# Three attention layers on one core: row maxima split before their transpose, one DMA of eight rows a unit, fewer idle matmuls before the second layer

## What is computed

```python
# block 0 (heads of 16, positional bias added to the scores), then layer norm
attn = softmax(q * scale @ k + pos[..., :, None] + pos[..., None, :])
x = layer_norm(x + w_proj @ (attn @ v) + b_proj)
# blocks 1 and 2 (heads of 32), group norm first
xn = group_norm(x) * gamma + beta
attn = softmax((xn @ wq.T + bq) * scale @ (xn @ wk.T + bk))
x = x + wo @ (attn @ (xn @ wv.T + bv)) + bo
# block 3
V = (Wv @ x + bv) * sigmoid(mean(Q * K)); energy = V @ (Ws @ x + bs).T
x = x + softmax(energy) @ (We @ x + be)
```

## Time and profile before

| | us |
|---|---|
| three timed runs | 490.71, 485.31, 489.66 |
| their median | 489.66 |
| the profiled execution | 484.69 |
| its span, first to last instruction | 483.0 |
| PE busy in the span | 455.1 (94%) |
| DVE busy | 362.9 (75%) |
| ACT busy | 267.4 (55%) |
| POOL busy | 214.8 (44%) |
| mean granted TensorE clock (1 is full) | 0.987 |

### The profile page before, as it was taken

The page is one execution under the profiler, slowest core; times in us unless marked ns, Lnnn a source line. Parts: engine busy times, 40 slices in busy tenths (PEclk is TensorE's granted clock), DMA queues, the critical chain, the costliest instruction groups (busy, mean ns, idle before and its releaser), DMA issues.

```text
span 483.0 us, 7045 instructions
## 1 busy us (share of the span) xinstructions
PE 455.1 (94%) x2228; PEld 233.9 (48%) x2228; DVE 362.9 (75%) x700; ACT 267.4 (55%) x515; POOL 214.8 (44%) x195
## 2 busy tenths in 40 slices
PE   8898999999896989999899999999999999999996
PEld 6544444444246576544444433656544444433463
DVE  7699877876578489977776756769987776748673
ACT  3228877777622327876766672124777665765032
POOL 8300031047310005889788941002799789980100
PEclk9979999999998999999999999999999999999999
DMA  5331525103210154488954441045377865452002
GB/s 154 55 59 26 155 50 134 34 4 66 47 21 0 29 126 115 90 201 178 203 115 86 92 78 24 1 97 127 82 156 153 173 116 107 76 103 47 0 2 87
DMA packets 20657, 41.88 MB, mean 87 GB/s; under 512 B 7458, under 2 KB 8746, under 8 KB 20364
## 3 DMA queue, kind: packets, MB, share of 16 engines
q1 hardware_dynamic: 15324, 25.41, 22.0%
q0 software_dynamic: 5152, 16.00, 18.0%
q10 hardware_dynamic: 144, 0.02, 0.0%
HBM read 5.94 MB, written 1.05 MB: 14 GB/s over the span
## 4 chain that ended last, share of the span: by engine, by line
PE 69%; SPq 11%; DVE 7%; DMA 4%; ACT 4%; POOL 3%; issue 2%; ACTq 0%; DVEq 0%; POOLq 0%
PE S L983 16%; PE PV L1021 15%; PE S L1010 15%; SPq L338 5%; SPq L331 4%; DMA k_stack<-kL 3%; PE PV L935 3%; PE S L1145 3%; ACT E L589 3%; DVE max L734 3%; POOL SUMS L525 2%; PE M L1034 2%; PE PV L961 2%; PE S L1179 2%; PE S L961 2%
## 5 line engine op out<-in xcount | busy, mean ns | idle before, releaser
L734 DVE TENSOR_REDUCE max<-S 128x1 f32<-128x512 f32 x384 | 238.8, 674 | 11.0 <-PE S L983 10.6
L589 ACT ACTIVATE E<-S 128x512 f32<-128x512 f32 x384 | 210.7, 607 | 54.2 <-PE S L1010 46.4
L525 POOL TENSOR_TENSOR SUMS<-E 128x512 f32<-128x512 f32 x120 | 158.9, 1437 | 108.5 <-ACT E L589 108.2
L983 PE MATMUL S<-k_stack,q_stack 126*128 126x512 f32 x384 | 176.8, 474 | 8.0 <-DMA k_stack<-kL 5.6
L1010 PE MATMUL S<-q_stack,k_stack 128*128 128x512 f32 x384 | 155.1, 413 | 5.5 <-ACT E L589 4.6
L983 PEld LDWEIGHTS S<-k_stack,q_stack 126*128 126x128 f32 x384 | 72.8, 191 | 78.7 <-DVE max L734 48.7
L1021 PE MATMUL PV<-E,V 128*32 128x512 f32 x768 | 91.6, 598 | 0.0
L1010 PEld LDWEIGHTS S<-q_stack,k_stack 128*128 128x128 f32 x384 | 72.3, 190 | 34.6 <-ACT E L589 20.0
L747 DVE TENSOR_TENSOR mHL<-S,mHL 4x128 fp32r<-4x128 f32 x48 | 13.3, 278 | 48.8 <-ACT mHL L578 48.8
L1021 PEld LDWEIGHTS PV<-E,V 128*32 128x32 f32 x768 | 20.7, 109 | 46.5 <-issue 27.2
L578 ACT ACTIVATE mHL<-S 4x128 fp32r<-4x128 f32 x48 | 12.6, 263 | 49.9 <-PE S L1001 49.9
(11 more groups left out here) (174 smaller groups left out, 336.9 us busy)
## 6 DMA issues: line engine op xcount, KB each, us to landing
SUMS<-SUMS POOLq DMA_DIRECT2D x30, 512.0 KB, 6.0
k_stack<-kH SPq DMA_DIRECT2D x28, 128.0 KB, 2.8
q_stack<-qH SPq DMA_DIRECT2D x40, 64.0 KB, 2.0
rec_sb<-den_sb SPq DMA_DIRECT2D x9, 256.0 KB
q_stack<-qH SPq DMA_DIRECT2D x16, 128.0 KB, 2.3
k_stack<-kL SPq DMA_DIRECT2D x14, 128.0 KB, 2.9
q_stack<-mHL SPq DMA_DIRECT2D x96, 2.0 KB
k_stack<-kH SPq DMA_DIRECT2D x22, 64.0 KB, 2.3
```

Of the source, the lines that this page charges most:

```text
L525: pool.tensor_tensor(SUMS[:, slot, :], E[:, E_PLAN[s][0], :], E[:, E_PLAN[s + 1][0], :], ALU.add).then_inc(sum_ready, 1)
L589: act.activation(E[:, slot, :], B[:, ring_of_scores(s) % B_RING, :], ACT.Exp, scale=1.0 if l == 0 else float(HEAD_DIM[l]) ** -0.5).then_in ...
L734: dve.tensor_reduce(max8[:, m % 2, 2 * t + half:2 * t + half + 1], A[:, n % A_RING, :], AX.X, ALU.max, negate=True).then_inc(a_used, 1)
L983: pe.matmul(A[:, n % A_RING, :], q_stack[0:SHIFT_ROW, slot, q0:q0 + P], k_stack[0:SHIFT_ROW, slot, k0:k0 + HALF], start=True, stop=True).t ...
```

## The change

**Row maxima.** The reductions of L734 no longer negate. After the eighth, DVE makes three small reductions instead of one, into `maxHL` (128 x 3 x 4): the exact maximum; the negated maximum rounded to fp32r (the high part); and the negated sum of these two, which is the low part. The third waits for the second by a semaphore. The transpose takes high and low together, 128 x 8 to eight rows. ACT copies the eight rows (`shift_out`), and SP writes them to both partitions of `q_stack` with one DMA. `low_rows` on DVE is gone, with its wait for ACT.

**Idle matmuls.** `keep_warm(14)` ahead of the second layer's first statistics matmul becomes `keep_warm(5)`. The third layer keeps 14.

```diff
-        negmax = sb("negmax", [P, 2, 4])
-        mHL = sb("mHL", [4, 2, 2, P], F32R)
+        mHL = sb("mHL", [8, 2, P], F32R)
+        maxHL = sb("maxHL", [P, 2, 3, 4], F32R)
...
-                for r in range(2):
-                    sp.wait_ge(rows_low if r else rows_high, m + 1)
-                    row = SHIFT_ROW + r
-                    sp.dma_start(q_stack[row:row + 1, slot_of(h), HALF * f:HALF * (f + 1)].bitcast(F32)
-                                 .rearrange("o (t c) -> o t c", t=4),
-                                 mHL[:, m % 2, r, :].bitcast(F32)).then_inc(shift_dma[m % 2], 16)
+                sp.wait_ge(rows_out, m + 1)
+                sp.dma_start(q_stack[SHIFT_ROW:P, slot_of(h), HALF * f:HALF * (f + 1)].bitcast(F32)
+                             .rearrange("r (t c) -> r t c", t=4),
+                             mHL[:, m % 2, :].bitcast(F32)).then_inc(shift_dma[m % 2], 16)
...
-                act.activation(mHL[:, m % 2, 0, :], B[0:4, ring_of_rows(j) % B_RING, 0:P], ACT.Copy).then_inc(rows_high, 1)
+                act.activation(mHL[:, m % 2, :], B[0:8, ring_of_rows(j) % B_RING, 0:P], ACT.Copy).then_inc(rows_out, 1)
...
-                    dve.tensor_reduce(negmax[:, m % 2, :], max8[:, m % 2, :].rearrange("p (t r) -> p t r", r=2), AX.X,
-                                      ALU.min).then_inc(negmax_ready, 1)
-
-            def low_rows(l, j):
-
-                m = UNITS_L * l + j
-                dve.wait_ge(rows_high, m + 1)
-                dve.tensor_tensor(mHL[:, m % 2, 1, :], B[0:4, ring_of_rows(j) % B_RING, 0:P],
-                                  mHL[:, m % 2, 0, :].bitcast(F32), ALU.subtract).then_inc(rows_low, 1)
+                    most, high, low = (maxHL[:, m % 2, part, :] for part in range(3))
+                    pairs = max8[:, m % 2, :].rearrange("p (t r) -> p t r", r=2)
+                    dve.tensor_reduce(most.bitcast(F32), pairs, AX.X, ALU.max).then_inc(max_split, 1)
+                    dve.tensor_reduce(high, pairs, AX.X, ALU.max, negate=True).then_inc(max_split, 1)
+                    dve.wait_ge(max_split, 3 * m + 2)
+                    dve.tensor_reduce(low.bitcast(F32), maxHL[:, m % 2, 0:2, :].bitcast(F32).rearrange("p a t -> p t a"),
+                                      AX.X, ALU.add, negate=True).then_inc(max_split, 1)
...
-                    if s in ROWS_AT:
-                        low_rows(l, ROWS_AT[s])
...
-                    pe.wait_ge(rows_low, UNITS_L * l + at + 1)
+                    pe.wait_ge(rows_out, UNITS_L * l + at + 1)
...
-                pe.transpose(B[0:4, ring_of_rows(j) % B_RING, 0:P], negmax[:, m % 2, :], ident[:, :]).then_inc(rows_done, 1)
+                pe.transpose(B[0:8, ring_of_rows(j) % B_RING, 0:P], maxHL[:, m % 2, 1:3, :].rearrange("p a t -> p (a t)").bitcast(F32),
+                             ident[:, :]).then_inc(rows_done, 1)
...
-                    keep_warm(14)
+                    keep_warm(5 if l == 1 else 14)
```

More of the change, by code:

```diff
@@ L196, in attention_chain @@
         a_done, a_used = sem("a_done"), sem("a_used")
-        negmax_ready, rows_done = sem("negmax_ready"), sem("rows_done")
-        rows_high, rows_low = sem("rows_high"), sem("rows_low")
+        rows_done = sem("rows_done")
+        max_split, rows_out = sem("max_split"), sem("rows_out")
         shift_dma = [sem(f"shift_dma{i}") for i in range(2)]
@@ L570, in project_out, with shift_out @@
                 act.activation(high, src, ACT.Identity, bias=bias, scale=scale).then_inc(high_ready, 1)
-            def high_rows(l, j):
+            def shift_out(l, j):
                 m = UNITS_L * l + j
@@ L576, in high_rows @@
                 if m >= 2:
-                    act.wait_ge(shift_dma[m % 2], 32 * (m // 2))
-                act.activation(mHL[:, m % 2, 0, :], B[0:4, ring_of_rows(j) % B_RING, 0:P], ACT.Copy).then_inc(rows_high, 1)
+                    act.wait_ge(shift_dma[m % 2], 16 * (m // 2))
+                act.activation(mHL[:, m % 2, :], B[0:8, ring_of_rows(j) % B_RING, 0:P], ACT.Copy).then_inc(rows_out, 1)
             def probabilities(l, s):
@@ L629, in _ @@
                     project_out(l, n)
-                high_rows(l, 0)
+                shift_out(l, 0)
                 for n in range(6, 8 if l else 6):
@@ L634, in _ @@
                     if s in ROWS_AT:
-                        high_rows(l, ROWS_AT[s])
+                        shift_out(l, ROWS_AT[s])
                     probabilities(l, s)
@@ L731, in maxima @@
                 if r == 0 and m >= 2:
-                    dve.wait_ge(negmax_ready, m - 1)
+                    dve.wait_ge(max_split, 3 * (m - 1))
                 t, half = maxima_tile(i)
-                dve.tensor_reduce(max8[:, m % 2, 2 * t + half:2 * t + half + 1], A[:, n % A_RING, :], AX.X, ALU.max,
-                                  negate=True).then_inc(a_used, 1)
+                dve.tensor_reduce(max8[:, m % 2, 2 * t + half:2 * t + half + 1], A[:, n % A_RING, :], AX.X,
+                                  ALU.max).then_inc(a_used, 1)
                 if r == TILES - 1:
@@ L998, in transpose_max @@
                 m = UNITS_L * l + j
-                pe.wait_ge(negmax_ready, m + 1)
+                pe.wait_ge(max_split, 3 * (m + 1))
                 ring_free(l, ring_of_rows(j))
-                pe.transpose(B[0:4, ring_of_rows(j) % B_RING, 0:P], negmax[:, m % 2, :], ident[:, :]).then_inc(rows_done, 1)
+                pe.transpose(B[0:8, ring_of_rows(j) % B_RING, 0:P], maxHL[:, m % 2, 1:3, :].rearrange("p a t -> p (a t)").bitcast(F32),
+                             ident[:, :]).then_inc(rows_done, 1)
             def scores(l, s):
@@ L1007, in scores @@
                 if t == 0:
-                    pe.wait_ge(shift_dma[m % 2], 32 * (m // 2 + 1))
+                    pe.wait_ge(shift_dma[m % 2], 16 * (m // 2 + 1))
                 ring_free(l, ring_of_scores(s))
```

## The result

| | before | changed |
|---|---|---|
| median of 13 runs, us | 488.39 | 482.54 |
| lowest, highest | 484.81, 491.54 | 480.7, 485.04 |
| profiled execution, us (mean granted clock) | 484.69 (0.987) | 485.04 (0.968) |

The ratio is 0.9878, 95% interval 0.9849 to 0.9908: 1.2% or 5.9 us faster. The two profiled executions don't show this, since that of before was the fastest of its kernel and that of after the slowest. Lines after the change: L732 large reductions, L740, L741 and L743 small ones, L977 and L1005 the two score matmuls, L1016 `values`, L1029 denominators, L995 the transpose, L523 GpSimd's sums.

What follows compares the result with a forecast made beforehand. It took DVE as the pace in the second half of each steady unit. Terms 6.0 + 0.8 + 1.6 + 0.3 + 1.0 = 9.7 us off gave 475.0 or 480.0 from two pairs of executions; middle 477.5, range 472 to 485.

Steps and rivals of the forecast that it cites:

- the likeliest case: The whole kernel: the forecast itself, all terms together giving 477.5 us, own range 473 to 482, chance 0.62.
- rivals A and B: Whole kernel: the two slower outcomes, each with its own line under Rival A and Rival B; chances 0.17 and 0.13.
- something unseen on the slow side: Whole kernel: an unnamed cause making it slower than forecast, no size given; chance 0.04.
- Part 1: Steady units: without `low_rows` DVE's third reduction comes earlier, 0.25 us in each of 24 units, 6.0 us off.
- Rival A: Steady units: DVE wasn't last; PE, ACT or POOL keeps the unit at 6.4 us; 481.0 or 483.5 us, chance 0.17.
- Part 2: DVE's two extra small reductions: free in steady units; in each layer's first five units, net 0.8 us off.
- Rival C: DVE, all 48 units: the split costs more than it frees, small reductions delaying large ones; 497 us, chance 0.04.
- Part 3: PE's transpose and ACT's copy, now of eight rows instead of four: no cost, taken as 0.
- Part 4: SP's single DMA a unit: 1.6 us off at two head 7 stalls, 0.3 at the first layer's shift rows.
- Part 5: Second layer's first statistics matmul: nine idle matmuls less let it start earlier, 1.0 us off.
- Rival B: Second layer's projections: the clock doesn't come back and they run at half clock; 484.2 us, chance 0.13.
- it could lag some hundredths a unit, with buffers between: POOL in steady units: needs 6.24 us a unit against the new period of 6.21, counted as no cost.

Runs made afterwards that it cites:

- e12: e4 with three more small reductions a unit on DVE, into a tile that nobody reads; 480.0 us, ratio 0.9829.
- e9: e5 with each unit's eight rows sent by two DMAs of four rows instead of one; 490.42 us, ratio 1.0063.
- e1: The changed kernel with 14 idle matmuls ahead of the statistics in both layers again; 484.68 us, ratio 0.9904.
- e7: e5 with 14 idle matmuls ahead of the statistics in both layers; 488.92 us, ratio 1.0001.
- e2: The kernel before with 5 idle matmuls instead of 14 ahead of the second layer's statistics, nothing else; 487.45 us, ratio 0.9949.
- e10: The changed kernel with the reciprocals written to 16 rows and spread over 128 partitions from these instead of from 4; 475.23 us, ratio 0.9744.
- e4: The changed kernel with the second block's spread of reciprocals cut to 64 of 512 columns in the last two layers; 475.89 us, ratio 0.9729.
- e13: The kernel before with the reciprocals spread from 16 rows, the same edit as e10; 487.33 us, ratio 0.9974.
- e3: The changed kernel with the third block's denominators four steps later, at step 115 instead of 111; 482.93 us, ratio 0.9863.
- e11: The changed kernel with the second block's spread issued only after unit 11's sums land, in the last two layers; 479.59 us, ratio 0.9828.
- e5: The changed kernel with the spread of the reciprocals made as four DMAs, one head each; 488.42 us, ratio 0.9998.

## Why the prediction was right and where it failed

The forecast was 477.5 us in a range from 472 to 485; the kernel takes 482.5. Faster by over 1% came true. The mechanism was right, and one cost was not seen. That the time lies in the range is in part luck: the likeliest case had its own range, 473 to 482, and the wider one reached to 485 for rivals A and B, of which A didn't come and B only in a small part. What came was the case called "something unseen on the slow side", which was given 0.04.

- **Part 1** held to a hundredth: unit 6.20 us for the 6.21 given, 0.54 us from load to reduction for 0.53. Summed over the transposes, without the stalls for head 7, the steady parts of the three layers gave 2.5, 1.9 and 2.0 us: 6.4 for 6.0. Rival A fell with it.
- **Part 2** held for the steady units: the three small reductions take 0.34 us for 0.35, and e12 shows that even three more are free there. My expectation for e12 forgot this own step. For the first units the net of 0.8 us off isn't seen: the lead shrinks by 0.2 us over those of the second layer (3.54 to 3.33) and of the third (1.01 to 0.79). The real share of DVE's waits for ACT was set too high, or the cost too low; no run tells which. Rival C fell all the same.
- **Part 3** held: 264 and 85 ns for eight rows, 263 and 83 for four.
- **Part 4** was probably sized too small: 1.6 + 0.3 us were given, e9 measures 3.2, but 1.1 to 5.3 holds the 1.9 too. I took 0.8 us for each stall of head 7; in the changed kernel's trace both are gone, 1.25 and 1.04 us, but in e1, e7 and e12 a part of them stays.
- **Part 5**, 1.0 us: e1, e2 and e7 give 1.3, 2.5 and 0.1 by medians, and 1.1, 1.6 and 1.7 in single executions up to the second layer's first transpose. Rival B in its full form (7 us) didn't come; a small part of it did (clock 0.89 in one execution).
- **The step that failed** is in part 1: "it could lag some hundredths a unit, with buffers between". It compared GpSimd's period with the unit's, and left out what stands behind it: the DMA that each unit's sums still need, and a fixed place in PE's order (step 111) that reads the result. There the kernel before had 10.4 us from issue to need for a transfer that took 9.4; in the changed kernel it took 10.7, with 2.4 us less room. No row of that place was read. The price was 6.5 to 7.3 us (e10 and e4), more than the 3.8 us between the sum of the terms and the result.

With that one wait taken away, the change is worth 11 us (8.6 to 14) by e10 and e13, or some 8 if e13's stall of 3.2 us is the edit's own, against the sum of 9.7. Middle of the pairs minus the sum was a fair base: the kernel before has a median of 488.39 over 13 runs, where the middle of the two pairs was 487.2.

That the clock's fall, and not the pause alone, is part of the 5.2 us at the second layer's end is read from the rows (3.64 us for 1.92) and wasn't tried by itself. Nor is it shown that the pause caused the fall: in e3, e11 and e12 the clock also fell to 0.50, at about 433 us in the third layer, behind waits of at most 0.5 us.

## What to carry to other kernels

When a unit gets shorter, check every fixed place in the order where one engine reads what another chain delivers: take the time from the transfer's issue to its use before the change, and ask whether the chain speeds up as much as its reader. A transfer without a wait in the profile may have next to no slack; here it was 1.0 us. And look at what else is on the DMA engines then: a broadcast from few partitions is slow for itself and holds up all that shares its engines, so read it from more rows; more engines on the same row made it worse here.

## What the hardware showed

- A broadcast within SBUF of 256 KB moved 49 GB/s from four rows (0, 32, 64, 96), with a DMA share of 0.24, and 193 from sixteen (every eighth), with 0.93. As four DMAs of one row each it moved 29 GB/s with a share of 0.94 (290 to 292 us of the changed kernel and e5; e10, 286 to 287).
- The same accumulating DMA of 512 KB, unit 11's, landed in 4.6 us (e4, where the spread was cut short), 5.5 (e11, where the spread came behind), 5.9 (e10, sixteen rows), 9.4 (kernel before) and 10.7 us (changed kernel, both with the four-row spread under way).
- Near the end of a pause of 2.8 us on PE the granted clock fell to 0.50 and stayed there for about 6.8 us (274.7 to 281.5); sixteen matmuls took 1.7 us more than at full clock.
- A small reduction (128 x 8 to 128 x 4, 0.15 to 0.16 us) costs DVE 0.06 to 0.08 us start to start, and 0.18 to 0.19 where the next one waits for it by a semaphore.
